# Heads by token tile, expert slots summed on GpSimd in six blocks instead of two, four of sixteen head pieces multiplied on VectorE

## The reference

```
x = x + attn_a(norm(x))        # causal attention with a latent
x = x + experts(norm(x))       # top 2 of 8, LoRA on every projection
x = x + heads(norm(x))         # RoPE, attention of the 16 heads of ONE token among each other
x = x + experts(norm(x))       # the same weights again
x = x + delta(norm(x)); x = x + ffn(norm(x)); x = x + attn_b(norm(x)); x = x + ffn(norm(x))
```

```
# experts, for each of the two chosen slots k with gate rw[k]:
x2   = silu(x @ W1.T + lora1(e_k)) * (x @ W3.T + lora3(e_k))     # 896 wide
out += (x2 @ W2.T + (x2 @ A2[e_k].T) @ B2[e_k].T) * rw[k]
# heads, for each token: q, k, v are 16 heads of 16
scores[h,t] = sum_d q[h,d] * k[t,d] / 4 ; w = softmax over t ; attn[h,d] = sum_t w[h,t] * v[t,d]
```

## Time and profile before

| what | value |
|---|---|
| median of 3 runs (lowest to highest) | 1299.37 us (1299.3 to 1304.58) |
| the profiled execution | 1299.7 us |
| its span, from the first to the last instruction | 1297.9 us |
| mean granted TensorE clock | 0.988 |
| instructions | 17678 |

### The profile page before, as it was taken

One profiled execution on the slowest core, in us unless ns is written; L12 is line 12 of the kernel. 1 busy time (PEld: TensorE's weight loads), 2 busy tenths in 40 slices (PEclk: granted clock), 3 DMA queues, 4 the chain that ended last, 5 costly groups with the idle time before them and its releaser, 6 DMA issues.

```text
span 1297.9 us, 17678 instructions
## 1 busy us (share of the span) xinstructions
PE 1185.8 (91%) x6873; PEld 912.7 (70%) x6873; DVE 677.1 (52%) x1661; ACT 417.7 (32%) x899; POOL 250.0 (19%) x161
## 2 busy tenths in 40 slices
PE   6889999999998989988787999999999989899888
PEld 5678675767867778667665786757678667786666
DVE  5754266664465556344634433666644655563452
ACT  3623031313322342433453431313133223424352
POOL 0002083650110210000000020836501102100000
PEclk9999999999999999999998999999999999999999
DMA  8200000000000000000000000000000000000000
GB/s 348 121 1 1 1 1 1 1 1 1 1 1 2 1 1 1 1 2 9 1 9 1 1 1 1 1 1 1 0 1 1 1 1 1 1 1 2 1 1 17
DMA packets 3570, 17.32 MB, mean 13 GB/s; under 512 B 288, under 2 KB 2464, under 8 KB 2976
## 3 DMA queue, kind: packets, MB, share of 16 engines
q1 hardware_dynamic: 2912, 14.12, 2.7%
q10 hardware_dynamic: 576, 2.08, 0.4%
HBM read 15.15 MB, written 1.05 MB: 12 GB/s over the span
## 4 chain that ended last, share of the span: by engine, by line
PE 69%; DVE 12%; issue 9%; ACT 6%; POOL 3%; DMA 0%; DVEq 0%; POOLq 0%; ACTq 0%
PE bank L704 65%; ACT scr L1311 3%; PE bank L721 2%; DVE XnT L2014 2%; DVE XnT L2016 1%; DVE scr L1590 1%; DVE stat L1582 1%; POOL rstd L2170 1%; DVE negmax L1672 1%; PE bank L822 1%; DVE X L1575 1%; PE bank L1122 1%; ACT scr L1289 1%; POOL fac L2170 1%; ACT XnT L1289 1%
## 5 line engine op out<-in xcount | busy, mean ns | idle before, releaser
L704 PE MATMUL bank<-pack,scr 128*128 128x256 f32 (+2 forms) x952 | 297.7, 464 | 9.4 <-ACT scr L1289 7.5
L704 PE MATMUL bank<-XnT,pack 128*128 128x256 f32 x1024 | 255.4, 390 | 12.3 <-ACT XnT L1289 7.1
L704 PEld LDWEIGHTS bank<-pack,scr 128*128 128x128 f32 x952 | 176.9, 190 | 104.2 <-issue 77.0
L704 PE MATMUL bank<-scr,pack 128*128 128x256 f32 x944 | 227.0, 380 | 1.3 <-DVE scr L1768 1.1
L704 PEld LDWEIGHTS bank<-XnT,pack 128*128 128x128 f32 x1024 | 194.2, 194 | 47.1 <-ACT XnT L1289 9.6
L704 PEld LDWEIGHTS bank<-scr,pack 128*128 128x128 f32 x944 | 178.1, 190 | 30.3 <-issue 4.4
L2205 POOL TENSOR_TENSOR scr<-scr 128x1024 f32<-128x1024 f32 x64 | 149.9, 2390 | 47.3 <-DVEq L1831 46.6
L2170 POOL TENSOR_TENSOR rstd<-veps,half 128x2 f32<-128x2 f32 x32 | 22.3, 698 | 627.1 <-DVE veps L1587 627.1
L1778 DVE TENSOR_TENSOR scr<-bank,scr 128x256 f32<-128x256 f32 x112 | 47.2, 423 | 149.7 <-ACT scr L1362 148.6
L1311 ACT ACTIVATE scr<-bank,negmax 128x256 f32<-128x256 f32 (+1 forms) x256 | 82.9, 445 | 92.8 <-DVE negmax L1672 92.8
L1362 ACT ACTIVATE scr<-bank 128x256 f32<-128x256 f32 x112 | 42.6, 385 | 210.8 <-PE bank L704 210.7
(11 more groups left out here) (184 smaller groups left out, 1406.3 us busy)
## 6 DMA issues: line engine op xcount, KB each, us to landing
pack<-pack_dram SPq DMA_DIRECT2D x1, 6152.0 KB, 17.2
pack<-pack_dram SPq DMA_DIRECT2D x1, 2180.0 KB, 29.2
pack<-pack_dram SPq DMA_DIRECT2D x1, 1595.0 KB, 23.3
X<-x SPq DMA_DIRECT2D x4, 256.0 KB, 16.8
pack<-pack_dram SPq DMA_DIRECT2D x1, 1024.0 KB, 20.2
pack<-pack_dram ACTq DMA_DIRECT2D x1, 975.5 KB, 6.2
pack<-pack_dram SPq DMA_DIRECT2D x1, 793.5 KB, 24.6
out_dram<-X SPq DMA_DIRECT2D x3, 256.0 KB, 2.1
```

Source lines behind the costliest of these rows:

```text
L704: return pe.matmul(o, l, r, start=start, stop=stop, skip_group_check=True)
```

## The change

- `joined(k, s)` is now true for `k == 0 or s % 2 == 0`: six of eight blocks, all but (1, b) of each half.
- `norm_x` 2, `norm_t` 2, `heads_in`, and for k = 0 `lora_t` and `lora`, work on one token tile each, so that a tile can go ahead. `rot_ready` is counted by tile. In block (0, a) the down products go tile by tile.
- `down` is cut in two stages, `down_half` (m = 0 to 2, which now claims the bank) and `down` (m = 3 to 6), with a slot between them.
- The head pieces stand at other slots, the same for a and b, and the last four (AHEAD = 12) are multiplied by VectorE itself, just before it sums them.

```diff
+AHEAD = PIECES - HP
...
         def joined(k, s):
 
-            return k == 0 and s % 2 == 0
+            return k == 0 or s % 2 == 0
...
+                                  "down01h": [("lora_t", 0, (0, 0))],
+                                  "down01": [("lora", 0, (0, 0)), ("norm_x", 2, (0, 0))]})
...
             weave[0] = True
+            stage("norm_t", 2, (a, 0))
             stage("x_first", 0, (b, 0))
-            stage("lora", 0, a)
-            stage("norm_x", 2, a)
-            experts(stage, 0, b, token_heads(a))
+            stage("lora", 0, (a, 1))
+            stage("norm_x", 2, (a, 1))
+            stage("heads_in", 0, (a, 0))
+            beside = token_heads(a)
+            beside["down11h"] = [("lora_t", 0, (b, 0))]
+            beside["down11"] += [("lora", 0, (b, 0))]
+            experts(stage, 0, b, beside)
             stage("router", 1, a)
-            stage("lora", 0, b)
+            stage("norm_x", 2, (b, 0))
+            stage("lora", 0, (b, 1))
             stage("spread_t", 1, a)
             stage("top_exp", 1, a)
             stage("spread", 1, a)
-            stage("norm_x", 2, b)
+            stage("norm_t", 2, (b, 0))
+            stage("norm_x", 2, (b, 1))
             stage("spread2", 1, a)
             stage("x_first", 1, (a, 0))
+            stage("heads_in", 0, (b, 0))
             stage("gates", 1, a)
             experts(stage, 1, a, token_heads(b))
...
             if s % 2 == 0:
-                beside = {"f2": [("norm_t", 2, s)], 2: [("heads_in", 0, s)]}
-                slots = ["f3", 3, "f4", 4, 4, "f5", 5, 5, "f6", 6, 6, "f7", 7, 7, 8, 8]
+                beside = {"f2": [("norm_t", 2, (s, 1))], 2: [("heads_in", 0, (s, 1))]}
+                slots = ["f1", 1, "f2", 2, 3, "f4", 4, "f5", 5, "f6", 6, "f7", 7, "f8", 8, 8]
             else:
-                beside = {"f0": [("norm_t", 2, s)], 0: [("heads_in", 0, s)]}
-                slots = [1, "f2", 2, "f3", 3, 3, "f4", 4, "f5", 5, 5, "f6", 6, 6, "f7", 7]
-            first = 2 if s % 2 == 0 else 0
-            beside[first] += [("head_prod", 0, (s, p)) for p in range(HP)]
+                beside = {"f1": [("norm_t", 2, (s, 1))], 1: [("heads_in", 0, (s, 1))]}
+                slots = ["f1", 1, "f2", 2, 3, "f4", 4, "f5", 5, "f6", 6, "f7", 7, "f8", 8, 8]
+            beside["f0"] = [("head_prod", 0, (s, p)) for p in range(HP)]
             for p, (slot, piece) in enumerate(zip(slots, pieces)):
                 beside.setdefault(slot, []).append(piece)
-                if p + HP < len(pieces):
+                if p + HP < AHEAD:
                     beside[slot].append(("head_prod", 0, (s, p + HP)))
...
-            for i in range(TOPK):
-                for a in range(NT):
-                    stage("down", k, (s, i, a))
-                    others(f"down{i}{a}")
+            tiles = [(i, a) for a in range(NT) for i in range(TOPK)] if k == 0 and s % 2 == 0 else \
+                [(i, a) for i in range(TOPK) for a in range(NT)]
+            for i, a in tiles:
+                stage("down_half", k, (s, i, a))
+                others(f"down{i}{a}h")
+                stage("down", k, (s, i, a))
+                others(f"down{i}{a}")
             summing[0] = False
-            stage("lora_t", k, s)
+            stage("lora_t", k, (s, NT - 1) if k == 0 else s)
...
+            def down_half(k, sia):
+                s, i, a = sia
+                r = (k, s)
+                wd = w3("m_down", FT)
+                if i == 0 and (r, 0, a) in summed:
+                    return
+                o = claim(pe, ("down", r, i, a))
+                for m in range(FT // 2):
...
             def lora_t(k, s):
+                if k == 0:
+                    s, a = s
+                    tile_t(("am2T", (k, s), a), am2[s][:, a, :], KER, 4 * a, (am2_ready[s], nth(s, 3, a + 1)))
+                    return
...
                 p = (NT + a) * HP + h
-                dve.wait_ge(hprod_ready[s], nth(s, PIECES, p + 1))
+                if p < AHEAD:
+                    dve.wait_ge(hprod_ready[s], nth(s, AHEAD, p + 1))
+                else:
+                    wait_drained(dve, ("bv", s, a))
+                    link(dve.tensor_tensor(prod[s][:, hh], *pv_pairs(s, a, hh), ALU.mult))
                 dve.tensor_reduce(c[:, hh], prod[s][:, hh], AX.X, ALU.add).then_inc(hprod_read[s], 1)
```

More of the change, by code:

```diff
@@ L51 @@
 SERIES = 8
-NORMS = 8
+NORMS = 7
 H1 = 1024
@@ L728, in group, with tile_t @@
                 return last
+            def tile_t(key, src, n, idle, ready):
+                o = claim(pe, key)
+                warm(o, idle)
+                pe.wait_ge(*ready)
+                for t in range(n):
+                    last = pe.transpose(o[:, t * P:(t + 1) * P], src[:, t * P:(t + 1) * P], ident)
+                last.then_inc(full[ring.bank(key)], 1)
             def norm_t(k, s):
+                if k == 2:
+                    s, a = s
+                    tile_t(("xnT", 2, s, a), tile_n[s][a], KD, 0, (tile_xn[s], nth(s, 2, a + 1)))
+                    return
                 idle = 13 if (k, s % 2) == (5, 0) else 0
                 transposes(("xnT", k, s), lambda t, a: Xn[s][:, a, t * P:(t + 1) * P], KD,
-                           idle, (xn_ready[s], nth(s, NORMS, k + 1)))
+                           idle, (xn_ready[s], nth(s, NORMS, k + (k < 2))))
             def proj(key, s, weights, tiles, per, k=KD):
@@ L939, in down @@
                 wd = w3("m_down", FT)
-                if ("down", r, i, a) in ring.at:
+                if (r, 0, a) in summed and i == 0:
                     return
-                o = claim(pe, ("down", r, i, a))
-                for m in range(FT):
+                o = bank[ring.bank(("down", r, i, a))]
+                for m in range(FT // 2, FT):
                     if i == 1 and a == 0:
@@ L1257, in ffn_half @@
                     last.then_inc(full[ring.bank(key)], 1)
-            table = dict(ratio=ratio, ratio_rows=nothing, head_prod=nothing, spread2=nothing, delta_sq=nothing, consts=nothing, top_exp=nothing, ffn_half=ffn_half, delta_expand=nothing, delta_diag=nothing, conv_tap=nothing, gates=nothing, down_sum=down_sum, angles=nothing, norm_x=nothing, norm_t=norm_t, latent=latent, kv=kv, kv_fold=kv_fold,
+            table = dict(ratio=ratio, ratio_rows=nothing, head_prod=nothing, down_half=down_half, spread2=nothing, delta_sq=nothing, consts=nothing, top_exp=nothing, ffn_half=ffn_half, delta_expand=nothing, delta_diag=nothing, conv_tap=nothing, gates=nothing, down_sum=down_sum, angles=nothing, norm_x=nothing, norm_t=norm_t, latent=latent, kv=kv, kv_fold=kv_fold,
                          scores=scores, weights=weights, values=values, values_t=values_t, out_in=out_in, out_proj=out_proj, router=router, spread_t=spread_t, spread=spread, x_first=x_first,
@@ new lines, in heads_in @@
+                wait_full(dve, key)
+                o = psum(key, 2 * NH, 8, 2)
+                for i, tab in enumerate((cos_t, sin_t)):
+                    for j in range(2):
+                        t = (rtmp, rtmp2)[a][s][:, i, :, :].rearrange("p h (j d) -> p h j d", j=2)
+                        ins = dve.tensor_tensor(t[:, :, j, :], o[:, :, :, j],
+                                                tab[:, a, :].unsqueeze(1).broadcast_to([P, 2 * NH, 8]), ALU.mult)
+                        if i * 2 + j < 3:
+                            link(ins)
@@ L2146, in angles @@
                 ins.then_inc(trig_in, 1)
-            table = dict(ratio=nothing, ratio_rows=ratio_rows, head_prod=nothing, spread2=spread2, delta_sq=delta_sq, consts=consts, top_exp=nothing, ffn_half=nothing, delta_expand=delta_expand, delta_diag=delta_diag, conv_tap=conv_tap, gates=gates, down_sum=nothing, angles=angles, norm_x=norm_x, norm_t=nothing, latent=latent, kv=kv, kv_fold=kv_fold,
+            table = dict(ratio=nothing, ratio_rows=ratio_rows, head_prod=nothing, down_half=nothing, spread2=spread2, delta_sq=delta_sq, consts=consts, top_exp=nothing, ffn_half=nothing, delta_expand=delta_expand, delta_diag=delta_diag, conv_tap=conv_tap, gates=gates, down_sum=nothing, angles=angles, norm_x=norm_x, norm_t=nothing, latent=latent, kv=kv, kv_fold=kv_fold,
                          scores=scores, weights=weights, values=values, values_t=values_t, out_in=nothing, out_proj=out_proj, router=router, spread_t=nothing, spread=spread, x_first=x_first,
```

148 lines of the change are left out of this document (100 added, 48 removed).

## The result

The changed kernel takes 1344.52 us (median of 4 executions, 1343.46 to 1345.3) against 1299.34 for the kernel before in the same job: **ratio 1.0343, interval 1.0324 to 1.0363, slower by 45 us**. The prediction said 1312 with a range up to 1324. The profiled execution took 1343.46, its span 1341.6, its mean clock 0.961 instead of 0.988.

A forecast was written before the change was run, and what follows sets the result against it. VectorE's queue was taken to end the heads in both blocks. Per half, 4.4 us at (1, a)'s transposes, 0.2 bank sharing and 1.6 clock make 6.2; two halves add 12.4 to 1299.7, giving 1312 us, range 1294 to 1324.

The forecast's parts named there:

- The bound: Blocks (0, b) and (1, a): VectorE's queue ends the heads while PE stands still some 6 us; chance 0.50, 1305 to 1319.
- The queue after m = 5: VectorE from x_first(5) to the heads' end: 24.0 us of work plus 1.7 of waits for GpSimd, 25.7 us.
- The border: Between blocks (0, b) and (1, a): the router starts 16.2 us after the heads' end instead of 12.04, net +3.3.
- In block (1, a): ratio +0.4, its late `ratio_rows` +0.7: Start of (1, a): with tile 1's copy +0.8 and three down_sum pairs -2.6, the terms before x_first(5).
- Moved work of `heads_in` is as long as before: On the way to block (1, a): moving `heads_in` does not change the length of its work.
- The clock: PE's waits, twice in each half: one clock drop per half taken, +1.6 us, between none and two.
- The sum: Whole kernel: 6.2 us per half, two halves +12.4 on the profiled 1299.7, giving 1312 us.
- GpSimd as the bound: Rival: GpSimd's queue starts late and down(1, 0) waits for sums; no separate chance, counted in the forecast's waits.
- PE as the bound: Rival: VectorE's queue after m = 5 is under 19.7 us, about -8 per half, 1284 us; chance 0.19.
- Port waits at their worst: Rival: subtraction, first division and multiplies wait for GpSimd, 28 us a block, second clock drop, 1324 us; chance 0.13.
- Washed out: Rival: multiply overpriced by the slope, no port waits (24.0 us a block), no clock drop, 1302 us; chance 0.18.
- The joining saves nothing: Rival on the joined blocks' down_sum: no saving; set against half the columns in half the time; no chance given.

The follow-up runs named there:

- e6: e2 with piece 13 moved behind the product of x_second(6) and 20 warming matmuls ahead of the wait in `head_out_t`: 1306.73 us, ratio 1.0039.
- e1: The changed kernel with `gates` of a staged ahead of `heads_in` of b's first tile: 1320.92 us, ratio 1.0155.
- e2: e1 with `ratio_rows` of both woven joined blocks also ahead of `heads_in`: 1312.77 us, ratio 1.0097.
- e3: The changed kernel with slots summed in two blocks as before: 1332.4 us, ratio 1.0245.
- e9: e6 without its 20 warming matmuls, piece 13 still moved: 1311.85 us, ratio 1.0102.
- e7: The kernel before with six joined blocks and nothing else: 1328.08 us, ratio 1.0215.
- e10: e1 with slots summed in two blocks as before and all pieces multiplied by GpSimd: 1306.94 us, ratio 1.0046.
- e8: The kernel before with (1, a) joined too and the last four pieces on VectorE for b alone: 1309.58 us, ratio 1.0054.
- e12: e8 with b's last three pieces moved behind the products of x_second(5) and x_second(6): 1298.12 us, ratio 0.998.

## Why the prediction was wrong, step by step

**The bound.** That VectorE's queue sets the end of the heads in both blocks, with PE standing still there, was right. The trace names GpSimd's last sum for the larger part of TensorE's wait (2.31 us, then 0.66 for VectorE), but that sum had itself waited 3.54 us for a product in VectorE's queue. VectorE of the changed kernel, the last multiply and its reduction:

```profile
205.03 1.30 DVE L1954 TENSOR_TENSOR scr<-scr 128x1024 f32<-128x1024 f32 x1
206.36 1.22 DVE L1955 TENSOR_REDUCE scr<-scr 128x64 f32<-128x1024 f32 x1
207.61 0.43 DVE L1959 TENSOR_TENSOR scr<-scr,bmax 128x256 f32<-128x256 f32 x1
```

**The queue after m = 5.** The forecast let x_first(5) end at 181.8 and the heads 25.7 us later, at 207.5; they ended at 208.04. That this fits so well is luck, for two errors cancel. The product comes at 184.57:

```profile
184.57 0.42 DVE L1860 TENSOR_TENSOR scr<-bank,scr 128x256 f32<-128x256 f32 x1 [4.49 <-ACT scr L1425]
```

So x_first(5) ended at about 184.0, 2.2 us late (1.62 of it the wait for the copy, which no term had), and the queue took 24.1 us, 1.6 less than forecast. The multiply, in no row of before, was priced at 1.22 by the slope and took 1.30, 1.22, 1.22 and 1.30. Port waits were 0.03 for the subtraction, 0.3 for the first division and at most 0.08 for a multiply in (0, b), less than the 1.7: where a multiply met one of GpSimd's sums, the sum waited. In (1, a) the subtraction waited 1.8. It depends on where in a piece it falls.

**The border.** Forecast from the heads' end to the router 16.2, measured 17.7 (208.04 to 225.74). The shared bank's wait (1.04) and the `lora_t` wait (0.74) are there, together 1.5 us smaller than forecast; what makes it longer all the same are the 2.7 us that `head_out` and the products behind it lose at half clock (7.28 against 4.54 in e6).

**The step that failed.** "In block (1, a): ratio +0.4, its late `ratio_rows` +0.7". Port waits were given only to the subtraction, the divisions and two multiplies of the heads, all of them two-input instructions as in the earlier trace rows. Moving `heads_in` ahead of `gates` was counted as "Moved work of `heads_in` is as long as before": what it releases on GpSimd, and what stands behind it on VectorE, was not followed. The trace has four waits of about 2 us each there and TensorE idle 8.51 us; e1 and e2 give 31.8 us back by moving those lines alone (the copy of block (0, b) among them). That is more than the two halves' idle time of 17 us. In the trace the x products behind it run at half clock (4.61 us from 252.89, 2.85 in e3) and the second tile's rotation comes late, so that GpSimd idles 9.58 us before its fifth piece; how the rest divides between these was not measured.

**The clock** was the other term too small: one drop of 1.6 us a half was taken. The trace has three a half (in the first, 0.50 from 206 to 214, 248 to 256 and 302 to 310). The two at `head_out_t`, which the forecast meant, cost 4 us a half by e6 and e9; the third belongs to the failed step.

**The sum.** With `gates` and `ratio_rows` ahead of the pieces, the kernel takes 1312.77, beside the predicted 1312, and in its trace the transposes of (1, a) come at 291.88 where 292.2 was forecast. Part of that agreement is luck: the clock costs 5 us more than was put in, and the queue in (0, b) took 24.1 us there too instead of 25.7.

**The rivals.** GpSimd as the bound was set aside because it had 38.7 us of work in 45. That holds for the changed kernel, where GpSimd idles 3.5 us for VectorE's product before its last two sums (202.87). In e7, with all 16 pieces on GpSimd and a later start, it is GpSimd that TensorE waits for, and the sums cost 2.2%. PE as the bound never came near in the change. "Port waits at their worst" had the mechanism and a price of 1324, but placed it at the softmax. "Washed out" had the port waits of (0, b) nearly right, and the clock wrong. "The joining saves nothing" was set aside by the earlier trace rows, half the columns in half the time; that holds for TensorE's work, but the time of the kernel with the sums, and with the multiplies that came with them, shows no saving (e2 beside e10).

## What to carry to other kernels

When a stage moves, follow what it releases on the other engines, and list every VectorE instruction that will now run beside GpSimd: any with two SBUF inputs, a copy or a `tensor_scalar` can cost a whole GpSimd instruction, down to 128x2 here, so put the small ones ahead of GpSimd's long work. Work taken from one engine is no gain where the queue of another sets the end, as e2 beside e10 shows; price the order of that queue's last entries (0.7% between e8 and e12) before the saving itself. And where TensorE will wait some microseconds, count the slower stretch after the wait too.

## What the runs showed of the hardware

- Beside GpSimd's 128x1024 multiplies (2.3 us each) a `tensor_scalar` of 128x2 took 2.34 instead of 0.16 us, a two-input instruction of 128x2 2.04 instead of 0.16, one of 128x16 2.26, and the 128x256 copy of `ratio_rows` in block (0, b) 2.46 instead of 0.29. The reciprocal (0.17), the reductions (1.21) and products with an input in PSUM (0.42) kept their length there.
- The wait can last longer than one GpSimd instruction: 5.86 us, over the ends of two pieces, once in the trace of e8.
- It goes the other way too: GpSimd's 128x256 sums beside VectorE's multiplies took 1.58 and 1.57 instead of 0.73 us (at 197.75 and 202.87 in the changed kernel).
- Twenty short matmuls put ahead of a wait kept the granted clock up behind it: 1.00 from 205 to 215 in e6, 0.69 from 208 to 216 in e9.
- The kernel before ran from 1294 to 1312 us in the later jobs, and the slower an execution, the lower as a rule its mean granted clock, 0.995 to 0.977; what makes the clock differ was not settled.
